# First group of an adaLN feed-forward kernel on Trainium2: x1 and y kept in PSUM, weight rests on one engine, plain numbering of y

## The reference

```python
q_emb = relu(cond @ W3 + b3)                       # 64 x 512
x1 = (n * x + sum_over_tokens(x)) * q_emb[:, None] # n = 64
y = relu(x1 @ W2 + b2)
base   = y @ W_base + b_base
shared = (y @ A_s) @ B_s                           # rank 16
gates  = softmax(y @ W_router + b_router)          # 6 experts, top 2 kept
h      = y @ A_r[e]                                # 6 experts, rank 16
routed = sum_e((h_e * w_e) @ B_r[e])
out = x + base + shared + routed
```

## Time and profile before

| | before |
|---|---|
| median of 3 runs | 243.40 us (243.38 to 243.43) |
| the profiled execution: its own time | 243.54 us |
| the profiled execution: span, first to last instruction | 241.8 us |
| TensorE busy | 233.5 us, 97% |
| VectorE, ScalarE, GpSimd busy | 175.7, 103.7, 50.1 us |
| granted TensorE clock | 1.00 throughout |

### The profile page before, as it was taken

How to read it: one execution, slowest core, us unless ns; L and a number is a source line. 1 busy time by engine, 2 the same in 40 slices (tenths; PEclk the granted TensorE clock), 3 DMA queues, 4 the chain that set the end, 5 groups by cost and what they waited for, 6 DMA issues and landing times.

```text
span 241.8 us, 3183 instructions
## 1 busy us (share of the span) xinstructions
PE 233.5 (97%) x1017; PEld 189.5 (78%) x1017; DVE 175.7 (73%) x325; ACT 103.7 (43%) x208; POOL 50.1 (21%) x56
## 2 busy tenths in 40 slices
PE   7998799999999999999999999999999999999994
PEld 3876588788878878888888888888888888888882
DVE  0598999699979987599756977589756986362334
ACT  2297672434435353326335354235435355224330
POOL 5099261003122230204102230204102230000000
PEclk9999999999999999999999999999999999999999
DMA  6999901754061765037800764027000620022004
GB/s 215 313 245 219 223 5 49 128 185 164 0 147 26 232 204 88 0 133 219 174 0 0 246 191 86 0 112 235 0 0 0 245 102 0 1 78 98 0 1 174
DMA packets 26266, 27.43 MB, mean 113 GB/s; under 512 B 2653, under 2 KB 17053, under 8 KB 26126
## 3 DMA queue, kind: packets, MB, share of 16 engines
q1 hardware_dynamic: 26018, 27.22, 39.9%
q10 hardware_dynamic: 236, 0.07, 0.1%
HBM read 18.89 MB, written 8.39 MB: 113 GB/s over the span
## 4 chain that ended last, share of the span: by engine, by line
PE 67%; DVE 25%; issue 3%; ACT 2%; POOL 1%; POOLq 0%; DVEq 0%; ACTq 0%
PE m_ps L726 57%; PE hT L726 6%; DVE xT L463 5%; DVE x_sum L475 3%; DVE vsum L468 3%; DVE x_lo L483 3%; DVE out_nat L605 3%; PE m_ps L704 2%; DVE y_lo L489 2%; DVE Wb_lo L526 1%; POOL x_full L306 1%; PE m_ps L717 1%; DVE x_full L508 1%; ACT Wb_hi L390 1%; DVE logit L538 1%
## 5 line engine op out<-in xcount | busy, mean ns | idle before, releaser
L306 POOL TENSOR_TENSOR x_full<-x_sum,qT 128x512 f32<-128x512 f32 x28 | 34.0, 1214 | 140.3 <-DVE x_sum L475 140.3
L726 PE MATMUL m_ps<-Wb_hi,y_hi 128*128 128x512 f32 x128 | 49.8, 389 | 0.0
L726 PE MATMUL m_ps<-Wb_hi,y_lo 128*128 128x512 f32 x128 | 49.8, 389 | 0.0
L726 PE MATMUL m_ps<-Wb_lo,y_hi 128*128 128x512 f32 x128 | 49.8, 389 | 0.0
L726 PE MATMUL m_ps<-x_hi,W_hi 128*128 128x512 f32 x112 | 43.9, 392 | 0.4 <-DVE x_lo L483 0.4
L726 PE MATMUL m_ps<-x_hi,W_lo 128*128 128x512 f32 x112 | 43.6, 389 | 0.0
L726 PE MATMUL m_ps<-x_lo,W_hi 128*128 128x512 f32 x112 | 43.6, 389 | 0.0
L353 ACT ACTIVATE y_full<-m_ps,b_sb 128x512 f32<-128x512 f32 x32 | 22.0, 687 | 48.8 <-PE m_ps L726 46.6
L489 DVE TENSOR_TENSOR y_lo<-y_full,y_hi 128x512 fp32r<-128x512 f32 x32 | 23.6, 738 | 12.4 <-ACT y_hi L355 12.4
L483 DVE TENSOR_TENSOR x_lo<-x_full,x_hi 128x512 fp32r<-128x512 f32 x32 | 24.1, 759 | 9.2 <-ACT x_hi L345 8.9
L463 DVE STREAM_TRANSPOSE xT<-x_quart 128x512 f32<-128x512 f32 x28 | 30.4, 1086 | 0.0
(11 more groups left out here) (94 smaller groups left out, 277.1 us busy)
## 6 DMA issues: line engine op xcount, KB each, us to landing
out_dram<-out_nat SPq DMA_DIRECT2D x32, 256.0 KB, 2.0
x_quart<-in_x_dram SPq DMA_DIRECT2D x28, 256.0 KB, 4.7
x_nat<-in_x_dram SPq DMA_DIRECT2D x7, 1024.0 KB, 6.3
x_nat<-in_x_dram SPq DMA_DIRECT2D x4, 256.0 KB, 3.4
W_f<-in_L_cond_W_dram SPq DMA_DIRECT2D x4, 256.0 KB, 7.4
Wb_f<-in_L_ffn_W_base_dram SPq DMA_DIRECT2D x1, 1024.0 KB, 10.2
W_sb<-in_L_cond_W_dram SPq DMA_DIRECT2D x1, 512.0 KB, 5.6
Ar_f<-in_L_ffn_A_r_dram SPq DMA_DIRECT2D x1, 192.0 KB, 5.8
```

Source lines behind the costliest of these rows:

```text
L306: nc.gpsimd.tensor_tensor(per_batch(x1_full[:, c, :]), per_batch(x1_sum[:, c, :]), qT[:, c, bass.ds(BG * g, BG)].unsqueeze(2).to_broadcast ...
L726: mm = nc.tensor.matmul(psum, lhsT, rhs, start=start and i == 0, stop=stop and i == len(terms) - 1)
```

## The change

In the first group the scaled x1 is written back to the PSUM bank it came from, and ScalarE (`x1_split_head`) and VectorE (`rest_head`) read it there. In every group ScalarE writes y_hi first and then y_full in place, into the m1 bank, and no longer waits for y_rest; VectorE's `y_rest` reads the bank. GpSimd makes all the weight rests: W2, Wd (one instruction over the full width) and all four of Wb. W2, W_base, A_s, A_r, the router and b2 are taken in plain numbering, so the loads are of smaller pieces: W_base 2 KB, A_r and A_s 64 B, router 24 B, b2 4 B. Wd_f, zeroed by GpSimd, takes the router, A_s and A_r. Half of A_r is issued by ScalarE after condT, W_base goes ahead of Wd in SP's queue, and b2 behind the quarters. The fourth q goes ahead of m1, in m1_ps[3]. The keep-warm products are 9 at the start, none between tiles, 4 at the end. ScalarE's order changes, and the copies to `pick` move behind Wu_hi in step 0.

```diff
-    WARM_LOAD, WARM_TILE, WARM_W3 = 7, 1, 5
+    WARM_LOAD, WARM_W3 = 9, 4
...
-        y_full = [sb(f"y_full{i}", [P, TG]) for i in range(2)]
+        Wd_f = sb("Wd_f", [P, KC, P])
...
-        q_ps = m1_ps[:KC - 1] + [m2_ps[0]]
+        q_ps = m1_ps
...
+        def load_A_r(eng, chunks):
+            for k in chunks:
+                eng.dma_start(Wd_f[:, k, RO:P].rearrange("p (e r) -> p e r", r=R),
+                              A_r[:, k * P:(k + 1) * P, :].rearrange("e p r -> p e r")).then_inc(Wd_loaded, 16)
...
-            sp.dma_start(Ar_f[:, :, :, :], A_r.rearrange("e (p k) r -> p e k r", k=KC)).then_inc(Wd_loaded, 16)
-            sp.dma_start(As_f[:, :, :], A_s.rearrange("(p k) r -> p k r", k=KC)).then_inc(Wd_loaded, 16)
-            sp.dma_start(Wr_f[:, :, :], W_router.rearrange("(p k) e -> p k e", k=KC)).then_inc(Wd_loaded, 16)
-            sp.dma_start(Wb_f[:, :, :], W_base.rearrange("(p k) d -> p k d", k=KC)).then_inc(Wb_loaded, 16)
-            sp.dma_start(b2_sb[:, :], b2.rearrange("(p m) -> p m", m=KC)).then_inc(b2_loaded, 16)
+            sp.dma_start(Wb_f[:, :, :], W_base.rearrange("(k p) d -> p k d", p=P)).then_inc(Wb_loaded, 16)
+            sp.wait_ge(zeroed, 3)
+            sp.dma_start(Wd_f[:, :, 0:E], W_router.rearrange("(k p) e -> p k e", p=P)).then_inc(Wd_loaded, 16)
+            sp.dma_start(Wd_f[:, :, SH:SH + R], A_s.rearrange("(k p) r -> p k r", p=P)).then_inc(Wd_loaded, 16)
+            load_A_r(sp, range(KC // 2, KC))
             load_quarters(1, 1)
-            sp.wait_ge(zeroed, 3)
+            sp.dma_start(b2_sb[:, :], b2.rearrange("(k p) -> p k", p=P), allow_slow_non_contiguous=True).then_inc(b2_loaded, 16)
+            sp.wait_ge(zeroed, 4)
...
-                W_rest(in_tiles(W2_lo[:, c, :]), by_tile(W2_f[:, c, :]), in_tiles(W2_hi[:, c, :]), W2_lo_ready)
-            for n, (lo, raw, hi) in enumerate(zip(Wd_parts(Wd_lo), Wd_raw, Wd_parts(Wd_hi))):
-                pool.wait_ge(Wd_hi_ready, n + 1)
-                W_rest(lo, raw, hi, Wd_lo_ready)
-            for k in range(KC // 2):
+                W_rest(W2_lo[:, c, :], W2_f[:, c, :], W2_hi[:, c, :], W2_lo_ready)
+            pool.wait_ge(Wd_hi_ready, 1)
+            W_rest(Wd_lo[:, :, :], Wd_f[:, :, :], Wd_hi[:, :, :], Wd_lo_ready)
+            for k in range(KC):
...
-                if not (first and m < 2):
-                    act.wait_ge(y_lo_ready, n - 1)
-                nc.scalar.activation(y_full[m % 2][:, :], m1_ps[m][:, :], ACT.Relu,
-                                     bias=b2_sb[:, m:m + 1]).then_inc(y_full_ready, 1)
                 nc.scalar.activation(y_hi[:, m, :], m1_ps[m][:, :], ACT.Relu,
                                      bias=b2_sb[:, m:m + 1]).then_inc(y_hi_ready, 1)
+                nc.scalar.activation(m1_ps[m][:, :], m1_ps[m][:, :], ACT.Relu,
+                                     bias=b2_sb[:, m:m + 1]).then_inc(y_full_ready, 1)
...
+            act.wait_ge(zeroed, 3)
+            load_A_r(act, range(KC // 2))
...
             q_relu(0)
             W2_split(0)
             q_relu(1)
-            x1_split(0, 0, 0)
+            x1_split_head(0)
             q_relu(2)
+            x1_split_head(1)
+            q_relu(3)
             W2_split(1)
-            x1_split(0, 0, 1)
             W2_split(2)
+            x1_split_head(2)
             W2_split(3)
-            x1_split(0, 0, 2)
-            q_relu(3)
-            act.wait_ge(Wd_loaded, 16 * 3)
-            for hi, raw in zip(Wd_parts(Wd_hi), Wd_raw):
-                nc.scalar.activation(hi, raw, ACT.Copy).then_inc(Wd_hi_ready, 1)
-            x1_split(0, 0, 3)
+            act.wait_ge(Wd_loaded, 16 * (2 + KC))
+            nc.scalar.activation(Wd_hi[:, :, :], Wd_f[:, :, :], ACT.Copy).then_inc(Wd_hi_ready, 1)
+            x1_split_head(3)
             act.wait_ge(Wb_loaded, 16)
...
-                nc.vector.tensor_tensor(per_batch(x1_full[:, c, :]), per_batch(head_ps[c][:, :]),
+                nc.vector.tensor_tensor(per_batch(head_ps[c][:, :]), per_batch(head_ps[c][:, :]),
...
+            def rest_head(c):
+                dve.wait_ge(x1_hi_ready, c + 1)
+                nc.vector.tensor_tensor(x1_lo[0][:, c, :], head_ps[c][:, :],
+                                        x1_hi[0][:, c, :].bitcast(F32), ALU.subtract).then_inc(x1_lo_ready, 1)
...
-            for k in range(KC // 2, KC):
-                dve.wait_ge(Wb_hi_ready, k + 1)
-                nc.vector.tensor_tensor(Wb_lo[:, k, :], Wb_f[:, k, :], Wb_hi[:, k, :].bitcast(F32),
-                                        ALU.subtract).then_inc(Wb_lo_back_ready, 1)
             dve.wait_ge(const_ready, 3)
...
-                        if k == 0 and m < KC - 1:
+                        if k == 0:
                             pe.wait_ge(qT_ready, m + 1)
...
-                    if k == 0:
-                        pe.wait_ge(x1_full_ready, 1)
-                        q(KC - 1)
...
-            for c in range(KC - 1):
+            for c in range(KC):
                 q(c)
```

More of the change, by code:

```diff
@@ L284, in _ @@
                                     base=0, pattern=[[1, E], [-1, E]], channel_multiplier=0).then_inc(const_ready, 1)
-            nc.gpsimd.memset(Wd_hi[:, :, E:SH].bitcast(F32), 0.0).then_inc(Wd_lo_ready, 1)
-            nc.gpsimd.memset(Wd_lo[:, :, E:SH].bitcast(F32), 0.0).then_inc(Wd_lo_ready, 1)
             nc.gpsimd.memset(w_pack[:, :, :].bitcast(F32), 0.0).then_inc(pick_step, 1)
@@ L370, in W2_split, with x1_split_head @@
                 act.wait_ge(W2_loaded[c], 16)
-                nc.scalar.activation(in_tiles(W2_hi[:, c, :]), by_tile(W2_f[:, c, :]), ACT.Copy).then_inc(W2_hi_ready, 1)
+                nc.scalar.activation(W2_hi[:, c, :], W2_f[:, c, :], ACT.Copy).then_inc(W2_hi_ready, 1)
+            def x1_split_head(c):
+                act.wait_ge(x1_full_ready, c + 1)
+                nc.scalar.activation(x1_hi[0][:, c, :], head_ps[c][:, :], ACT.Copy).then_inc(x1_hi_ready, 1)
             q_relu(0)
@@ L392, in _, with pick_round @@
             act.wait_ge(bias_loaded, 16)
-            act.wait_ge(pick_step, 5)
-            for q in range(NQ):
-                nc.scalar.activation(pick[q * S:(q + 1) * S, :], pick_one[:, :], ACT.Copy).then_inc(pick_ready, 1)
+            def pick_round():
+                act.wait_ge(pick_step, 5)
+                for q in range(NQ):
+                    nc.scalar.activation(pick[q * S:(q + 1) * S, :], pick_one[:, :], ACT.Copy).then_inc(pick_ready, 1)
             def w_spread(g):
@@ L486, in y_rest @@
             def y_rest(g, m):
-                dve.wait_ge(y_hi_ready, KC * g + m + 1)
-                nc.vector.tensor_tensor(y_lo[:, m, :], y_full[m % 2][:, :],
+                dve.wait_ge(y_full_ready, KC * g + m + 1)
+                nc.vector.tensor_tensor(y_lo[:, m, :], m1_ps[m][:, :],
                                         y_hi[:, m, :].bitcast(F32), ALU.subtract).then_inc(y_lo_ready, 1)
@@ L515, in _ @@
             scale_head(1)
-            x1_rest(0, 0, 0)
+            rest_head(0)
             sum_head(2)
             scale_head(2)
-            x1_rest(0, 0, 1)
+            rest_head(1)
             sum_head(3)
             scale_head(3)
-            x1_rest(0, 0, 2)
-            x1_rest(0, 0, 3)
-            for k in range(KC // 2, KC):
-                dve.wait_ge(Wb_hi_ready, k + 1)
-                nc.vector.tensor_tensor(Wb_lo[:, k, :], Wb_f[:, k, :], Wb_hi[:, k, :].bitcast(F32),
-                                        ALU.subtract).then_inc(Wb_lo_back_ready, 1)
+            rest_head(2)
+            rest_head(3)
             dve.wait_ge(const_ready, 3)
@@ L720, in _ @@
                         turn.then_inc(head_turned, 1)
-                keep_warm(WARM_TILE if t < TT - 1 else WARM_W3)
+            keep_warm(WARM_W3)
             def product(psum, terms, start, stop):
@@ L787, in h @@
                 if k == 0 and first:
-                    pe.wait_ge(Wd_lo_ready, 2 + 3)
+                    pe.wait_ge(Wd_lo_ready, 1)
                 elif k == 0:
@@ L803, in m2 @@
                 if first and t == 0:
-                    if k < KC // 2:
-                        pe.wait_ge(Wb_lo_ready, k + 1)
-                    else:
-                        pe.wait_ge(Wb_lo_back_ready, k + 1 - KC // 2)
+                    pe.wait_ge(Wb_lo_ready, k + 1)
                 product(m2_ps[t][:, :], [(y_hi[:, k, toks], Wb_hi[:, k, :]),
```

13 lines of the change are left out of this document (2 added, 11 removed).

## The result

Median of four runs 239.88 us (239.78 to 240.09), beside 243.39 us (243.11 to 243.43) for the kernel before on the same chip: ratio 0.9859, 95% interval 0.9842 to 0.9877. That is 3.5 us faster. The forecast was 243.3 us with a range of 242.0 to 245.4, so it was wrong, in size and in the case chosen. The profiled execution took 239.78 us, its span 237.6 us, and 2.2 us lie around it.

What follows compares the result with a forecast made beforehand. The prediction took the start of TensorE's steady stretch, set by when VectorE can begin turn(0), as the bound. That moves by -0.06 and the rest hides: 243.54 - 0.06 - 0.14 = 243.3 us, range 242.0 to 245.4.

Steps and rivals of the forecast that it cites:

- T: Time at which VectorE can begin turn(0), the next group's first chunk; 24.60 before; each us moves the kernel's end by one.
- the step behind it: VectorE's transpose, sum, add and y_rest(0) after turn(0) begins; TensorE resumes with the y_lo product 3.19 us later.
- T is 22.84 + 1.70 = 24.54: Next group's last x_quart load, landing at 22.84, delayed 1.7 us by 4096 small packets for 1152; 0.06 before the old 24.60.
- Nothing that the change does ... in a steady group can show in the time.: From 28.13 us TensorE's queue covers VectorE, ScalarE and GpSimd; y_full in PSUM, ReLU order and dropped wait count nothing.
- First group's x1: With one operand in PSUM, VectorE's x_lo takes 0.69 us; the last two took 1.59 together before.
- Only 0.4 of it is left: Of up to 2 us that VectorE could gain at the end of x1, since x1_hi(3) holds it.
- W_base's pieces at nothing: Wb load as 512 packets of 2 KB instead of 128 of 8 KB: same bytes, no cost.
- Cover of the rests: GpSimd's weight rests finish in time, last Wb_lo by 26.5, over one us before m2 needs it.
- Start and m1: TensorE's first group: m1 starts about 12.9 instead of 12.58 and ends about 24.5 instead of 25.54, hidden by the y_lo wait.
- Cheap packets: Rival, chance 0.28: small-packet cost falls nearly with bytes, x_quart loads land soon after 22.84, up to 1.76 us gained, 241.6.
- VectorE keeps the lead: Rival, given nothing: x1_lo(3) at 20.8 sets T, m1's end bounds instead, about 240.5.
- Late quarters: Rival, chance 0.35: queue limits packets whatever their size, x_quart loads come late; 244.5, or 248.2 at 451 packets per us.

Runs made afterwards that it cites:

- those 1536 packets: Kernel after with half of A_r loaded again to a scratch tile, 64 B pieces, ahead of group 1's x_quart loads: 241.22 us, 0.9927.
- the six other kernels with the old loads: Kernel before with all rests on GpSimd, x1 in PSUM, y in PSUM, three y_full buffers, y_hi first, or the first three together: 239.90 to 243.3 us.
- the runs with SP's wait: SP waits for group 1's quarters before later loads: before plus GpSimd rests 241.83 us; after 239.75; before plus GpSimd rests, x1 and y in PSUM, keep-warm 239.82.

## Why the prediction was wrong

**That T sets the end, and the step behind it.** Right. TensorE went on at T + 3.20 for a foretold T + 3.19, and extra packets moved T and the time alike. VectorE waits for the quarters with x_lo at 0.69, as said.

**"T is 22.84 + 1.70 = 24.54".** This step failed; T was 21.85. The 1.70 as an amount of work was sound, since 64 B measured 11 ns or more. The Trainium skill's beats and cycles (DMA: Bandwidth & Descriptors, Why small descriptors are slow) gave 7 ns as an estimate, 0.67 us for those 1536 packets; the run shows at least 1.06, and the measurement decides. What it was added to was wrong in two ways. First, 22.84 is one execution's landing at its late end: the six other kernels with the old loads landed between 21.2 and 22.3, in the middle at 21.3, so some 1.5 us of the error is there. Second, 1.70 is a mean over 16 engines, and it was added to the landing of the last part. Before the change the engines end unevenly; the added packets moved the 8th of the last sixteen parts by about what was forecast (19.6 to 20.7 in the six, 21.61 after), but the last part only from some 21.3 to 21.75, which is the other 1.3 us. That the engines end unevenly before and together after is shown by the runs with SP's wait; which of the moved loads evens them stays open. The 850 packets of group 2 that ran ahead before are a sign of the same unevenness, and that they delay the landing is not shown.

**"Nothing that the change does ... in a steady group can show in the time."** Wrong by more than one us. 0.66 us of pauses in 206 us was read as no pauses at all, and the sum over the whole stretch hid that TensorE waits for VectorE's chain at 43.35: what shortens the work behind T on VectorE, y_rest and what GpSimd's clashes with it delay, brings that forward too. y in PSUM alone gave 1.4 us with T unmoved, and 1.1 to 1.2 by time less T. The row that showed it was in the trace of the kernel before: y_lo at 1.53 us beside GpSimd's multiply. The prediction saw the same in x_lo, 1.32 against 0.69, and did not carry it to y_lo.

The two errors add up: 2.69 us of T and 1.01 of time less T are 3.70, the distance from the forecast for the profiled execution (243.48) to its 239.78; between the medians it is 3.4.

**First group's x1.** The 0.69 was right. "Only 0.4 of it is left" was too little: x1_hi(3) came at 16.92, not 20.1, since Wd was in by 16.4 and not 18.8. It did not matter, as the quarters bound.

**W_base's pieces at nothing.** Not refuted: 8 KB gave at most 0.6 us in the kernel after, not clear of the noise, and nothing in the kernel before. **Its place** was given no price, which was wrong: behind A_r it cost 1.6 us.

**Cover of the rests.** Right with more room: the last Wb_lo ended at 23.4, foretold 26.5. **b2** was there by T + 0.20, foretold 0.3 to 0.5.

**Start and m1.** m1 began at 11.88, one us sooner than the 12.9 worked out, and h started at 24.47 for a foretold 24.5. That agreement is by chance: the clock fell to 0.50 and took the lead back. "1.00 throughout" in the profile of the kernel before was chance too: in 41 of 54 other executions of it the mean granted clock was 0.991 to 0.993, as in the kernel after, and their median time was 243.1 us against 243.4 for the ten at full clock. The fall cost them nothing.

**The rivals.** "Cheap packets" had the sign and 241.6 as its end, but not the mechanism, for packets were not cheap. "VectorE keeps the lead", 240.5, is nearest in number, but its mechanism did not occur either: the quarters, not x1_lo(3), set T, and m1's end did not set the time. It was given no chance with the reason that the quarters would have to come earlier than they did; they came 1.1 us earlier, not two. "Late quarters" was wrong: 451 packets per us was no ceiling, as 9239 packets went through in 20 us, 462 per us on average, 3494 more small ones than before.

## What to carry to other kernels

Before adding a delay to a landing, take the landing from several executions, and look at how evenly the DMA engines end: a load is in when its last part is, and the added packets here filled engines that had stood idle, so they moved the mean by what was forecast and the end by little. Look for steps of one form with two durations (0.68 and 1.53 us): where VectorE reads two SBUF operands beside GpSimd, leaving one in PSUM removes the slow one, and on GpSimd too. When one event sets the time, compare runs by time less that event: the scatter of T, 0.9 us between kernels that should not differ, hid effects that were then constant to 0.1 or 0.2 us.
